# Two attention layers issued head by head, with half steps of projection work and matmuls of ones in their loops

## The reference

```python
# layer 1: 16 heads of 16, 256 queries, 256 keys (the context), boolean mask
x = layer_norm(hidden, ln1_w, ln1_b)
q = (x @ q_w + q_b).reshape(B, 256, 16, 16); k, v from the context
scores = where(mask, q k^T / 4, min); attn = softmax(scores)
out = (attn v) @ cproj_w + cproj_b + hidden; out = out + mlp(layer_norm(out))
# layer 2: 16 heads of 16, 256 queries (the latents), 512 keys: context and latents
h = concatenate([x, latents], axis=1)
attn = softmax(where(full_mask, q k^T / 16, -inf)); out = (attn v) @ out_w + out_b + latents
out = mlp(rmsnorm(out)) + latents
# layer 3: 32 query heads of 8 on 8 key heads, 256 keys, additive mask, then a layer norm
```

## Time and profile before

| what | value |
|---|---|
| median of three runs | 1412.97 us |
| profiled execution, its time | 1412.02 us |
| its span, first to last instruction | 1410.7 us |
| busy: PE, DVE, ACT, POOL | 1289.9, 903.1, 721.6, 547.4 us |
| loop of layer 1 and the drain behind it | 719 to 855 us |
| loop of layer 2 and the drain behind it | 916 to 1117 us |
| loop of layer 3 to the end | 1180 to 1411 us |

### The profile page before, as it was taken

One profiled execution on the slowest core, in us unless ns is written; L12 is line 12 of the kernel. 1 busy time (PEld: TensorE's weight loads), 2 busy tenths in 40 slices (PEclk: granted clock), 3 DMA queues, 4 the chain that ended last, 5 costly groups with the idle time before them and its releaser, 6 DMA issues. The chain is left out here.

```text
span 1410.7 us, 26853 instructions
## 1 busy us (share of the span) xinstructions
PE 1289.9 (91%) x9901; PEld 1098.9 (78%) x9901; DVE 903.1 (64%) x2341; ACT 721.6 (51%) x1817; POOL 547.4 (39%) x1003
## 2 busy tenths in 40 slices
PE   7999999999999999998977787978888898999995
PEld 6999999999999999997865556855554587666663
DVE  6866767688856767687765657455556375465661
ACT  4866666677756666576214443235444522444442
POOL 3544544445444545453443325043323131223332
PEclk9999999999999999999986889968997798899997
DMA  5320000023200000022012101220120112011000
GB/s 166 105 69 1 2 1 5 2 68 112 62 2 1 2 1 1 1 71 92 24 47 72 48 2 46 69 77 25 50 70 1 50 42 79 17 37 56 13 3 16
DMA packets 44132, 56.69 MB, mean 40 GB/s; under 512 B 10016, under 2 KB 24416, under 8 KB 44000
## 3 DMA queue, kind: packets, MB, share of 16 engines
q1 hardware_dynamic: 38880, 54.40, 12.3%
q0 software_dynamic: 5120, 0.56, 0.3%
HBM read 32.68 MB, written 1.05 MB: 24 GB/s over the span
## 5 line engine op out<-in xcount | busy, mean ns | idle before, releaser
L1797 ACT ACTIVATE PT<-bank 128x512 f32<-128x512 f32 x320 | 174.2, 595 | 165.5 <-PE bank L1739 84.2
L1078 POOL TENSOR_SCALAR E<-E,rl 128x256 f32<-128x256 f32 x256 | 238.1, 941 | 0.0
L1903 POOL DMA_DIRECT2D Q<-rows x160 | 90.3, 566 | 216.4 <-ACT rows L1811 208.5
L1076 POOL TENSOR_TENSOR pb<-E,rl 128x2 f32<-128x2 f32 x128 | 33.7, 263 | 327.4 <-DVE rl L954 327.4
L821 ACT ACTIVATE QTh<-bank,bqs 128x256 fp32r<-128x256 f32 x128 | 60.7, 474 | 182.6 <-PE bank L117 182.6
L1861 DVE CUSTOM_DVE_ANT_0 Em<-bank,M 128x256 bf16<-128x256 f32 x256 | 95.2, 420 | 75.7 <-issue 45.5
L1854 DVE TENSOR_REDUCE nm<-bank 128x1 f32<-128x512 f32 x128 | 82.3, 685 | 74.2 <-PE bank L1708 73.7
L831 ACT ACTIVATE E<-bank,nm 128x257 f32<-128x257 f32 x256 | 119.3, 480 | 3.1 <-DVE nm L931 3.1
L938 DVE SCALAR_TENSOR_TENSOR QTl<-bank,bqs,QTh 128x256 fp32r<-128x256 f32 x128 | 61.8, 483 | 85.3 <-ACT KT L822 84.4
L1754 PE MATMUL bank<-PT,V 128*32 128x256 f32 x1280 | 103.7, 462 | 2.6 <-ACT PT L1797 2.6
L1731 PE MATMUL bank<-Q,K 51*128 51x256 f32 (+1 forms) x640 | 97.4, 319 | 6.3 <-ACT PT L1797 5.4
(11 more groups left out here) (465 smaller groups left out, 4505.5 us busy)
## 6 DMA issues: line engine op xcount, KB each, us to landing
stage<-in_wts SPq DMA_DIRECT2D x99, 256.0 KB, 3.1
Q<-stage SPq DMA_DIRECT2D x72, 128.0 KB
K<-stage SPq DMA_DIRECT2D x48, 128.0 KB
K<-xh SPq DMA_DIRECT2D x16, 128.0 KB, 2.9
Q<-rows POOLq DMA_DIRECT2D x96, 4.0 KB, 1.7
K<-stage SPq DMA_DIRECT2D x24, 64.0 KB
X<-in_x SPq DMA_DIRECT2D x4, 256.0 KB, 6.0
stage<-in_ctx SPq DMA_DIRECT2D x4, 256.0 KB, 3.6
```

The source lines that it names most:

```text
L1078: m = pool.tensor_scalar(s.E[:, i % 3, t, 0:256], s.E[:, i % 3, t, 0:256], s.rl[:, r, t:t + 1], None, ALU.mult)
L1797: act.activation(s.PT[i % s.NPT][:, 2 * u:2 * u + 2, :].rearrange("p a b -> p (a b)"), s.STB[y][:], ACT.Exp).then_inc(S["t_ex"])
L1903: pool.dma_start(f32(s.Q[b % s.NR][at:at + 2, pair:pair + n, :]), f32(s.rows[4 * n * y:4 * n * y + 4 * n, g % 2, :])).then_inc(S[f"dma_row ...
```

## The change

All three loops are counted in finer steps, each with its own distance between the parts (`LAG`, `TURN`, `MEET`), but only layers 1 and 2 get another order.

- Layer 1: a step is one head instead of a pair. TensorE alternates between the scores by query of one head and those by key of the head 13 earlier.
- Layer 2: a step is one unit of a pair. The scores of y = 0 stand at the start of a step, those of y = 1 behind the weights by key and the attend.
- Preparation and closing work are cut in halves of 6 matmuls (`k0`, `k1`, ...) and spread over 16 steps of a batch instead of 8 pairs. An attend is cut in two parts, in successive steps. ScalarE's and VectorE's share of a preparation (`kh`, `kl`) has a step of its own in layer 1.
- Layer 3 keeps pairs and distances; its `q`, `k` and `v` move by a step or two, and a scores-by-key matmul of y = 0 no longer waits for the exponential of y = 1.
- `KEPT`: layer 1 has 8 tiles `PT` instead of 6.
- `keep_busy` issues four matmuls of ones (bf16, 128 x 128 by 128 x 256) into the bank `OB` at the start of a step, in layers 1 and 2, in those two of four steps in which no attend is open or waiting for its copy; before the first attend in every step. The program has 75 such groups, 39 in layer 1 and 36 in layer 2, 300 matmuls in all.

```diff
 RING = {1: (3, 3), 2: (2, 2), 3: (2, 2)}
 
+
+WIDTH = {1: 1, 2: 2, 3: 2}
+LAG = {1: 13, 2: 7, 3: 5}
+
 GROUP = {1: 4, 2: 2, 3: 4}
-DELAY = {1: 6, 2: 4, 3: 5}
+TURN = {1: 3, 2: 1, 3: 1}
+
+MEET = {1: (2, 2), 2: (1, 2), 3: (1, 1)}
+
+KEPT = {1: 8, 2: 6, 3: 6}
...
-IN_LAYER = {1: {0: ["mask", "k", "stats"], 1: ["v0", "k_out", "norm", "maskrow"], 2: ["turn", "scale"],
-                3: ["parts", "mask_out"], 4: ["q"], 5: ["q_out"]},
...
+IN_LAYER = {1: {0: ["mask", "k0", "stats"], 1: ["k1", "kh"], 2: ["kl", "norm"], 3: ["k_out", "maskrow"],
+                4: ["turn", "scale", "mask_out"], 5: ["v0", "th"], 6: ["v1", "va", "tl"], 8: ["q0"], 9: ["q1", "qh"],
+                10: ["ql"], 11: ["q_out"]},
...
+POSTS = {1: [["po0", "on0"], ["po1", "on1"], ["onT", "oth"], ["otl"], ["c0"], ["c1", "y"]],
+         2: [["po0", "on0"], ["po1", "on1"], ["onT", "oth", "otl"], [], ["c0"], ["c1", "y"]],
...
-    def turns_at(self, p):
-
-        last = 2 * p - self.G
-        return [last // self.G] if last >= 0 and last % self.G == 0 and p <= self.N else []
-
-    def attends_at(self, p):
-
-        v = p - self.D - 1
-        return [v // 2] if 0 <= v < self.N and v % 2 == 1 else []
+    def turns_at(self, n):
+
+        g, r = divmod(n - TURN[self.l] + 1, self.G * self.units // self.WD)
+        return [g - 1] if r == 0 and 0 < g <= 2 * self.N // self.G else []
+
+    def attends_at(self, n):
+
+        off, parts = MEET[self.l]
+        g, k = divmod(n - self.L - off + 1, self.four)
+        m = self.nkt // parts
+        return [(g - 1, m * k + e) for e in range(m)] if 0 < g <= self.N // 2 and k < parts else []
...
+    def by_query(n):
+
+        p, u, y = s.unit(n)
+        q, r = p % s.P, p // s.P % s.NR
+        at = slice(64 * y, 64 * y + s.R)
+        w.wait_ge(S["t_mx"], s.o["mx"] + (n - 1) * (2 if l == 3 else 1))
+        if l == 2:
+            pe.matmul(s.SB[y][:], s.Q[r][at, q, u * 128:u * 128 + 128], s.K[r][at, q, :], start=True, stop=True
+                      ).then_inc(S["t_s"])
+            return
+        for e in range(2):
+            z = pe.matmul(s.SB[y][:, 256 * e:256 * e + 256], s.Q[r][at, q, 128 * e:128 * e + 128],
+                          s.K[r][at, q // s.rp, :], start=True, stop=True)
+        z.then_inc(S["t_s"])
+
+    def by_key(n, e):
+
+        p, u, y = s.unit(n)
+        q, r, g = p % s.P, p // s.P % s.NR, 2 * p // s.G
+        at, o = slice(64 * y, 64 * y + s.R + 2), (2 * u + e) * 128
+        w.wait_ge(S[f"dma_rows{g % 2}"], 32 * ((s.o["g"] + g) // 2 + 1))
+        w.wait_ge(S["t_ex"], s.o["ex"] + n - 1)
+        if n < 2:
+            w.wait_ge(S["m_x"], 4 * (l - 1) + 2)
+        z = pe.matmul(s.STB[y][:, 256 * e:256 * e + 256], s.K[r][at, q // s.rp, o:o + 128], s.Q[r][at, q, :],
+                      start=l != 3 or e == 0, stop=l != 3, skip_group_check=l == 3)
+        if l != 3 and e == 1:
+            z.then_inc(S["t_st"])
...
+    def queries(n, y):
+
+        if y == 0 and n < s.T and n % s.TB == 0:
+            ready(n // s.TB)
+        if y == 0 and n < 2:
             w.wait_ge(S["m_gelu"], 16 * l)
-        for y in range(2):
-            at = slice(64 * y, 64 * y + s.R)
-            if l == 2:
-                w.wait_ge(S["t_mx"], s.o["mx"] + 4 * p + 2 * t + y - 1)
-                pe.matmul(s.SB[y][:], s.Q[r][at, q, t * 128:t * 128 + 128], s.K[r][at, q, :], start=True, stop=True
-                          ).then_inc(S["t_s"])
-            else:
-                w.wait_ge(S["t_mx"], s.mx(2 * p + y - 1))
-                for e in range(2):
-                    z = pe.matmul(s.SB[y][:, e * 256:e * 256 + 256], s.Q[r][at, q, e * 128:e * 128 + 128],
-                                  s.K[r][at, q // s.rp, :], start=True, stop=True)
-                z.then_inc(S["t_s"])
-
-    def weights_by_key(p, u):
-
-        b, q, r = p // s.P, p % s.P, p // s.P % s.NR
-        g, n = 2 * p // s.G, (p * s.units + u) * 2
-        w.wait_ge(S[f"dma_rows{g % 2}"], 32 * ((s.o["g"] + g) // 2 + 1))
-        if p == 0:
-            w.wait_ge(S["m_x"], 4 * (l - 1) + 2)
+        for k in s.in_step(n)[y:y + 1]:
+            by_query(k)
...
+    def keep_busy(n):
+
+        off, parts = MEET[l]
+        g, k = divmod(n - s.L - off + 1, s.four)
+        if l == 3 or n < 2 or n >= s.T or g > 0 and 0 < k <= parts:
+            return
+        w.wait_ge(S["m_x"], 4 * l)
+        w.wait_ge(S["t_os"], s.o["os"] + max(0, g if k else g - 1))
+        for _ in range(4):
+            pe.matmul(s.OB[:, 0:256], c.units[:, 0:128], c.units[:], start=True, stop=True)
+
+    for n in range(s.steps()):
+        keep_busy(n)
+        queries(n, 0)
+        if l == 3:
+            queries(n, 1)
+        keys(n - s.L)
+        for g in s.turns_at(n):
             turn_maxima(g)
-        for gi in s.attends_at(p):
-            attend(gi)
-        b, steps = s.preps(p)
+        for gi, k in s.attends_at(n):
+            attend(gi, k)
+        if l == 2:
+            queries(n, 1)
+        b, steps = s.posts_at(n)
+        for x in steps:
+            heads_post_pe(c, s, b, x)
+        b, steps = s.preps(n)
         for x in steps:
             heads_prep_pe(c, s, b, x)
...
-    for p in range(s.steps()):
-        if p < s.N:
-            maxima(2 * p, 0)
-            if l == 2:
-                maxima(2 * p + 1, 0)
-        b, steps = s.preps(p - 1)
+    for n in range(s.steps()):
+        for k in s.in_step(n)[:s.WD - 1]:
+            maxima(k)
+        b, steps = s.preps(n - 1)
...
+        for k in s.in_step(n)[s.WD - 1:]:
+            maxima(k)
```

More of the change, by code:

```diff
@@ L1143 @@
+POSTS_MLP = [["po0", "on0"], ["po1", "on1"], ["onT", "oth", "otl"], ["c0", "c1", "y"]]
+NEXT_NORMS = {0: [(0, "stats")], 1: [(0, "norm")], 3: [(0, "turn"), (0, "scale")], 5: [(0, "parts")],
+              7: [(1, "stats")], 8: [(1, "norm")], 10: [(1, "turn"), (1, "scale")], 12: [(1, "parts")]}
 class Heads:
@@ L1154, in __init__ @@
         self.N = NB * self.P
+        self.WD = WIDTH[l]
+        self.TB = 2 * self.P * self.units // self.WD
+        self.T = NB * self.TB
+        self.four = 4 * self.units // self.WD
         self.R = 3 * d + (0 if l == 3 else 1)
@@ L1465, in tokens_free @@
                 w.wait_ge(S["pe_v1"], b)
[L1467 removed]
+    if x == "th" and l == 1:
         w.wait_ge(S["h_hf"], b + 1)
@@ L1742, in attend @@
-    def attend(gi):
+    def by_query(n):
[7 more added lines that the diff above has]
+            return
+        for e in range(2):
+            z = pe.matmul(s.SB[y][:, 256 * e:256 * e + 256], s.Q[r][at, q, 128 * e:128 * e + 128],
+                          s.K[r][at, q // s.rp, :], start=True, stop=True)
+        z.then_inc(S["t_s"])
@@ L1743, in attend, with keys @@
+    def keys(n):
+        if l == 3:
+            for e in range(2):
+                for k in s.in_step(n):
+                    by_key(k, e)
+            for k in s.in_step(n):
+                add_mask(k)
+        else:
+            for k in s.in_step(n):
+                by_key(k, 0)
+                by_key(k, 1)
+    def attend(gi, k):
         b, g = gi // (nh // 4), gi % (nh // 4)
@@ L1751, in attend @@
             w.wait_ge(S["m_x"], 4 * (l - 1) + 3)
-        for k in range(nkt):
-            for q in range(4):
-                z = pe.matmul(s.OB[32 * q:32 * q + 32, 0:256], s.V[b % s.NV][:, k, (4 * g + q) // s.rep, :],
-                              s.PT[(i0 + q) % s.NPT][:, k, :], start=k == 0, stop=k == nkt - 1, skip_group_check=True)
-        z.then_inc(S["t_pv"])
+        for q in range(4):
+            z = pe.matmul(s.OB[32 * q:32 * q + 32, 0:256], s.V[b % s.NV][:, k, (4 * g + q) // s.rep, :],
+                          s.PT[(i0 + q) % s.NPT][:, k, :], start=k == 0, stop=k == nkt - 1, skip_group_check=True)
+        if k == nkt - 1:
+            z.then_inc(S["t_pv"])
     def turn_maxima(g):
@@ L1907, in heads_pool @@
     heads_ones(c, s, 1)
-    for p in range(s.steps()):
-        for g in s.turns_at(p - 1):
+    for n in range(s.steps()):
+        for g in s.turns_at(n - 1):
             maxima_rows(g)
-        for g in s.turns_at(p):
+        for g in s.turns_at(n):
             maxima_parts(g)
-        if p == 2 and max(s.NR, s.NV) > 2:
+        if n == 4 and max(s.NR, s.NV) > 2:
             heads_ones(c, s, 2)
-        b, steps = s.preps(p - 1)
+        b, steps = s.preps(n - 1)
         for x in steps:
             heads_prep_pool(c, s, b, x)
-        b, steps = s.posts_at(p - 1)
+        b, steps = s.posts_at(n - 1)
         for x in steps:
             heads_post_pool(c, s, b, x)
-        for b, x in s.norms(p - 1):
+        for b, x in s.norms(n - 1):
             if x == "stats":
```

305 lines of the change are left out of this document (141 added, 164 removed), and 5 rows, old and new, of the table IN_LAYER.

## The result

The changed kernel takes 1425.63 us (median of 20 runs, 1414.94 to 1433.52), the kernel before 1414.41 (20 runs, 1408.93 to 1420.8). The ratio is 1.0067, with a 95% interval from 1.0046 to 1.0087. I had predicted 1379 and faster; 1425.6 lies above the range, and the sign is wrong.

The account below looks back on a forecast made before the run. TensorE and VectorE waiting on each other over two banks, with a lowered TensorE clock, were taken as the bound. Terms -18 - 13 - 4 + 1 = -34 us gave 1379 against the median of 1412.97; 8-in-10 range 1346 to 1411.

Parts of the forecast that it names:

- What bounds the kernel: Loops of layers 1 and 2: TensorE and VectorE hand two banks to and fro; 40% of the time at 1.2 GHz.
- The ones: Layers 1 and 2: 300 matmuls, 0.48 us a group at full clock, 36 us of TensorE; count as work for the clock.
- Layer 2, -18 us: Layer 2's maxima, first to last: TensorE becomes the bound, mean clock 0.97, 161 us instead of 179.
- the turn's new wait: Layer 2: turned maxima wait for GpSimd's np; half of 6 us added a batch, 5 to 15 us to be seen.
- TensorE's content, 130 us: Layer 2's loop: TensorE's own work, 36.2 us a full batch, with y = 1's scores priced at 0.24 each.
- rival 3: No difference: finer order only moves waits, 36.2 + 6 is 42.2 against 40.7 a batch; about 1410, chance 0.12.
- Two more signs: VectorE's maxima in layers 1 and 2 would wait for score matmuls under half of 42 and 74 us.
- Layer 1, -13 us: Layer 1's maxima: finer order, TensorE and VectorE nearly equal, clock 0.94; 101 us instead of 114.
- the long norm near the start: Layer 1: one long norm stays near the start, beside GpSimd's memory setting; +4 us for the stall.
- The rest: Drains behind both loops -2 us each, together -4; layer 3 +1, lasting 229 to 235 us; MLP stages the same.
- Rival 1: Clock does not rise, ones are pure load: layer 2 +17 us, layer 1 no gain, 1429; chance 0.13.
- Rival 2: TensorE simply full and always fast, no added waits in layer 2: -74 us, named 1345; chance 0.15.

Follow-up runs that it names:

- e7: Kernel before, order untouched, plus 37 groups of eight matmuls of ones in pairs of layers 1 and 2 without an attend: 1395.63 us, 0.9871.
- e3: Changed kernel with the turn of layer 2's maxima two steps later (TURN 3 instead of 1), ones kept: 1395.35 us, 0.9866.
- e12: Changed kernel with the turn of layer 2's maxima one step later (TURN 2 instead of 1): 1394.88 us, 0.9872.
- e4: Changed kernel with layer 2's scores of y = 1 right behind those of y = 0 at the step's start, ones kept: 1386.32 us, 0.9803.
- e9: e5 with layer 1 set back to pairs, their distances and work lists, and 19 groups of eight ones there: 1382.65 us, 0.9783.
- e5: Changed kernel with layer 2's scores of y = 0 and y = 1 together and its maxima turned two steps later, ones kept: 1380.79 us, 0.9763.
- e1: Changed kernel without its 300 matmuls of ones: 1456.15 us, 1.0169.
- e6: e5 without the ones: 1396.75 us, 0.9877.
- e2: Changed kernel with ones in layer 1 only (156 of the 300 matmuls): 1443.41 us, 1.0205.
- e10: e5 with eight matmuls of ones in each of the 75 groups instead of four: 1399.57 us, 0.99.
- e8: Changed kernel, same number of ones, layer 2's groups of even steps right before the turned maxima instead of at step start: 1412.28 us, 0.9977.

## Why the prediction was wrong

**What bounds the kernel.** That the two engines hand banks to and fro, and that the clock was down 40% of the time, stood. The clock's share was read rightly for layer 1. For layer 2 e7 says otherwise: clock 0.89 for 0.81, and no time gained. Whether the exchange of banks is the bound there, or the ones cost what the clock gives, these runs do not tell apart.

**The ones.** The price was about right: a group of four, from 993.06 to the next instruction at 993.60 in the changed kernel, is 0.54 us at full clock, where I had 0.48. That they count as work for the clock was right. That they would be enough for it in layer 2 was not.

**Layer 2, -18 us: this is the step that failed.** It gave the turn's new wait half of the 6 us added to a batch, 12 us in the loop, and "5 to 15 us" as what would be seen. The wait came to 18 to 19, 15 or 16 times over. That alone is a miss of 6. The larger error is in what I took to follow from it, a clock of 0.97 beside a wait that stops the queue of the bounding engine again and again. The clock came to 0.80, and y = 1's scores behind the turn passed the wait on to VectorE (75 waits). With the measured clock my own sum gives 130/0.80 + 24 + 3 = 190 us: 29 of the 47 us between 161 and 208 are the clock, and 18 the longer wait and the dearer scores. e3 and e12 show the turn's part: one or two steps more return 30 us. In e4, which returns 39, the overlap of the scores is in it. That the clock falls behind these waits rests on where it falls in the traces and on its rise in e3 and e12; since other falls have another occasion, how much of it is theirs is an estimate.

What I called TensorE's content, 130 us, was too low too. The term mis-sized is the score of y = 1 by itself, 0.24 us: fifteen times between 950 and 1016 us of e3 it takes 0.42 or 0.43. There, at full clock and with the turn repaired, this many maxima were started:

```profile
950.00:1016.00 66.00, 34.06 (x51) 1.00 0.13 40
```

That is 1.29 us each, as slow as the 1.27 of the kernel before; 36.2 us for 32 would be 1.13. TensorE waited for only 2.5 of the 66 us, which leaves 1.25 of its own work for each. With the 6 us a batch that I had added for waits, the sum was 42.2 / 32 = 1.32, so that this pace came out nearly right by two errors that cancel. The changed kernel at 0.97, in the same stretch:

```profile
950.00:1016.00 66.00, 29.49 (x44) 0.97 0.17 52
```

1.50 us each, 14% above that 1.32 with hardly a fall of the clock, and 6.0 us of this stretch are waits for `np`. I had 1.27 of before in hand, and rival 3 had said that 42.2 against 40.7 is no gain.

Two more signs that I had named failed. VectorE's waits for scores should have been under half of 42 and 74 us; they are 24.3 and 96.9.

**Layer 1, -13 us.** The clock came as predicted (0.94), and so did the long norm near the start: 4.89 us for two, beside GpSimd's memory fills, where it was 4.71.

```profile
726.82 4.89 DVE L154 TENSOR_SCALAR xn<-X,bnmv,bnrs 128x256 f32<-128x256 f32 x2 [1.92 <-POOL bnrs L144]
```

Measured -7.6 from first to last maximum. The term had counted on the finer order and on the clock. e7, with the old order and ones, went from 112.9 to 100.2 at 0.97; e9, with the old order too, took 104.5 at 0.93, and e5, with the new one, 103.6 at 0.95. Without ones the new order took 107.5 at 0.75 (e1) and 113.2 at 0.67 (e6). So with ones both orders gain, and what the finer order gives by itself is not told apart from the clock. The error here is of size only: 105.3 us at 0.92 where I had 101 at 0.94.

**The rest.** Drains -5.1 for -4, layer 3 at 229 us for "229 to 235", -2.2 for +1: near enough. In part that is luck. The drains were measured together with the stages behind them, and came to +1.3 and -6.4 where I had -2 each; layer 3 takes from 219.5 (e2) to 226.7 us (e1) in kernels in which its code is the same.

**The rivals.** Rival 1 gave 1429 and came within 4 us of the result, and by its own sign it was on: the clock of layer 2 is under 0.87. But half of its mechanism is refuted. It had the ones as pure load and layer 1 without a gain. Taking them out costs time in every order tried (14 to 31 us here, 16 in e5's), and layer 1 has the clock. The other half stood: a clock of 0.80 in layer 2, and its argument that ones in the same queue can't fill a hole, since they wait too (e1: `np` is waited for as long without them). Its number, with layer 1 at no gain and layer 2 at +17, is right by errors that cancel. I had weighed it at 0.13, with "content per step rises" against it; more content did not keep the clock up.

Rival 3 (1410) had the pace right: at nearly full clock e3 starts a maximum every 1.29 us, the kernel before every 1.27, and e5 every 1.32:

```profile
950.00:1016.00 66.00, 33.06 (x50) 0.97 0.21 58
```

So by these paces the finer order itself gave nothing in layer 2, and what e5 gains there goes with its clock (0.96 for 0.81). Rival 2 (1345), no added waits and always fast, is out by both. The 1357 that I gave for half of its 74 us is a slip: half of it is 1376.

**Left open.** How far the clock would hold in the changed order if only the 5.47 us at the layer's start were gone (GpSimd's fills first or elsewhere) was not tried, nor why it falls there before that hole. Nor is it shown why e5's layer 2 takes 165.6 us and not about 129, which my content (130 less 9 for the scores together, at 0.96, and 3 for the start) would give; VectorE waits 57 us for scores there and TensorE 13 for maxima, so both sides still wait.

## What to carry to other kernels

When an operand comes through a chain over two other engines, leave a step between its last input and the matmul that reads it, and price such a wait with all that stands behind it in the queue and with the clock that may follow, not by its own length. Filler matmuls (here the ones) are worth a trial of their own, apart from a new order: on the old one they gave 19 us, and doubling them in a kernel that already had its clock cost 19. Before two matmuls that overlap are taken apart, read what one of them costs alone in the place where it will stand. A prediction that needs a full clock in a stretch should point to the waits it adds there and say why none of them brings it down.

## Not expected of the hardware

- The share of time that TensorE is listed busy does not tell the clock. In the loop of layer 2 e5 has 146.20 of 167 us (88%) and a clock of 0.96, the changed kernel in its stretch 196.31 of 226 (87%) and 0.79, and e3, with 170.64 of 181 (94%), only 0.88. What differs between the first two is how the idle time lies: 15 waits for `np`, 18.0 us, up to 5.5 at a time, against 19 for maxima, 13.0 us, up to 1.4, and two for `np`, 2.9 us. That this is what the clock answers to is not shown. Once low, it can also stay low while TensorE is listed full: e3 has 12.00 busy of 12 us from 926 to 938, at 0.50. The Trainium skill (TensorE: Matmul & The Clock Gate, Part 1, "A second HAM failure mode: psum-queue depth-cycling") tells of a kernel whose clock swings because TensorE idles briefly and often between groups of matmuls; the changed kernel agrees (0.79, with most of its waits for `np` under 2 us), but e5, which has as much idle time, hardly falls (0.96).
- 300 matmuls without any use, 36 us of the busiest engine, made a kernel faster by 16 us (e5 against e6); the next 300 made it slower by 19 (e10 against e5).
- The executions of one kernel differ in their mean clock, and the time follows it: e1 took 1433.06 us at 0.91 and 1469.37 at 0.879, e8 1403.68 at 0.962 and 1426.48 at 0.939, about 1 us for each thousandth. The kernels with the lowest clock in layer 2 (e1 with 0.61 and e2 with 0.63) scatter most.
